# Value products of an attention tile: one block of 512 queries in place of two of 256

## The reference, cut to what matters

```python
logits = jnp.einsum('bhsd,bhtd->bhst', q, k) / (math.sqrt(Dh) * T)
att = jax.nn.softmax(logits, axis=-1)
out = jnp.einsum('bhst,bhtd->bhsd', att, v)
...
q = (jnp.einsum('bld,ed->ble', x, Wq) + bq).reshape(b, l, h, dh)
kv = (jnp.einsum('bmc,ec->bme', y, Wkv) + bkv).reshape(b, m, h, 2 * dh)
k, v = (kv[..., :dh], kv[..., dh:])
att = jax.nn.softmax(jnp.einsum('blhd,bmhd->blmh', q, k) * scale, axis=2)
out = jnp.einsum('blmh,bmhd->blhd', att, v).reshape(b, l, d)
```

## Time and profile before

| | |
|---|---|
| median of 3 runs | 1681.13 us (1680.69 to 1683.37) |
| profiled execution, span from first to last instruction | 1681.4 us |
| attention stage in it | about 130 to 1253 us |
| value products | x7424, 592.8 us busy, mean 391 ns |
| scores | x1856, 565.8 us busy, mean 382 ns |
| products for the maxima | x2048, 534.1 us busy, mean 358 ns |
| exponentials | x1856, 1001.7 us busy, mean 598 ns |
| maxima | x928, 1049.3 us busy, mean 1198 ns |

### The profile page before, as it was taken

The page is one execution under the profiler, slowest core; times in us unless marked ns, Lnnn a source line. Parts: engine busy times, 40 slices in busy tenths (PEclk is TensorE's granted clock), DMA queues, the critical chain, the costliest instruction groups (busy, mean ns, idle before and its releaser), DMA issues. The chain is left out here.

```text
span 1681.4 us, 36595 instructions
## 1 busy us (share of the span) xinstructions
PE 1598.4 (95%) x14449; PEld 634.1 (38%) x14452; DVE 1499.6 (89%) x2182; ACT 1319.1 (78%) x2590; POOL 406.3 (24%) x666
## 2 busy tenths in 40 slices
PE   6999999999999999999999999999989999889997
PEld 3542222222223232223322222222235555657774
DVE  6899999989999999989899999999948887688876
ACT  4618999879988989898899999999985565545544
POOL 5800110212223312312211111111013443533302
PEclk9999999999999999999999999999999999999999
DMA  4001001001101200101221011010002000015551
GB/s 147 14 7 20 14 14 14 14 14 22 31 14 21 45 14 14 33 17 27 70 55 26 14 21 20 14 27 14 14 28 63 1 1 1 1 31 95 101 102 51
DMA packets 148026, 52.32 MB, mean 31 GB/s; under 512 B 137424, under 2 KB 146128, under 8 KB 147600
## 3 DMA queue, kind: packets, MB, share of 16 engines
q1 hardware_dynamic: 147152, 48.62, 14.1%
q10 hardware_dynamic: 704, 1.38, 0.2%
HBM read 14.07 MB, written 2.10 MB: 10 GB/s over the span
## 5 line engine op out<-in xcount | busy, mean ns | idle before, releaser
L968 DVE TENSOR_REDUCE mxp<-ps_m 128x2 f32<-128x1024 f32 (+2 forms) x928 | 1049.3, 1198 | 41.3 <-PE ps_m L747 39.9
L897 ACT ACTIVATE work<-ps_s 128x512 f32<-128x512 f32 x1856 | 1001.7, 598 | 76.7 <-PE ps_s L771 48.9
L797 PE MATMUL ps_av<-work,vst 128*32 128x256 f32 x7424 | 592.8, 391 | 14.7 <-ACT avs L904 12.3
L771 PE MATMUL ps_s<-qb,k_stack 50*128 50x512 f16 x1856 | 565.8, 382 | 0.5 <-ACT v_rows L915 0.3
L747 PE MATMUL ps_m<-k_stack,qa 48*128 48x512 f16 (+1 forms) x2048 | 534.1, 358 | 2.3 <-PEq L1123 0.5
L797 PEld LDWEIGHTS ps_av<-work,vst 128*32 128x32 f32 x7424 | 147.0, 108 | 383.2 <-ACT work L897 321.6
L771 PEld LDWEIGHTS ps_s<-qb,k_stack 50*128 50x128 f16 x1856 | 119.7, 94 | 378.6 <-ACT work L897 323.4
L747 PEld LDWEIGHTS ps_m<-k_stack,qa 48*128 48x128 f16 x2048 | 108.2, 93 | 21.5 <-DVE mxp L968 14.8
L616 POOL TENSOR_SCALAR mtmp<-negm 128x16 f32<-128x16 f32 x32 | 8.2, 255 | 390.5 <-DVE negm L973 390.4
L602 POOL COPY vst<-v_rows 128x1024 f32<-128x1024 f32 (+1 forms) x32 | 30.6, 956 | 144.5 <-PE ps_av L797 144.5
L682 POOL TENSOR_TENSOR q_rows<-avs,rc 128x256 f32<-128x256 f32 x31 | 19.2, 619 | 173.3 <-DVE rc L979 173.3
(11 more groups left out here) (441 smaller groups left out, 2006.1 us busy)
## 6 DMA issues: line engine op xcount, KB each, us to landing
x_res<-in_x SPq DMA_DIRECT2D x4, 512.0 KB, 8.2
w_experts<-in_w_experts SPq DMA_DIRECT2D x1, 2048.0 KB, 8.0
out<-x_res SPq DMA_DIRECT2D x8, 256.0 KB, 2.2
v_rows<-in_ctx_c SPq DMA_DIRECT2D x1, 1664.0 KB, 7.3
work<-in_ctx_t SPq DMA_DIRECT2D x1, 1456.0 KB, 15.8
ctx_n<-in_ctx_n SPq DMA_DIRECT2D x1, 1248.0 KB, 8.0
w_qkv<-in_w_qkv ACTq DMA_DIRECT2D x1, 768.0 KB, 8.6
w_qkv<-in_w_qkv SPq DMA_DIRECT2D x1, 768.0 KB, 4.2
```

What stands on the lines that cost most here:

```text
L771: pe.matmul(ps_s[:, bank, :], STACKS[part(n)][rows, group(n) * PAIRS + j, t * P:t * P + P], qb[n % 2][rows, :, j, :], start=True, stop=Tru ...
L797: m = pe.matmul(ps_av[32 * h:32 * h + 32, cols], vst[n % 2][:, t, h, :], pbuf[(tau[n] + t) % 2][:, h, cols], start=(t == 0 and half == 0), ...
L897: a.activation(pbuf[g % 2][:, h, :], ps_s[:, b, :], ACT.Exp, scale=factor).then_inc(s["exp"], 1)
L968: v.tensor_reduce(dst, src, AX.X, ALU.max).then_inc(s["mred"], 1)
```

## The change

`values` loses its argument `half` and covers all 512 queries. The call between the two pairs of scores is gone; the call after the second pair remains. The semaphore `av` then counts one per tile in place of two, and every wait for it is adapted.

```diff
             def values(n):
 
                 k = keys_of(n)
                 if n >= 2:
-                    g.wait_ge(s["av"], 2 * tau[n - 1])
+                    g.wait_ge(s["av"], tau[n - 1])
...
-            def values(n, t, half):
+            def values(n, t):
 
                 pe.wait_ge(s["exp"], scored[n, t])
-                if t == 0 and half == 0:
+                if t == 0:
                     pe.wait_ge(s["vst"], n + 1)
                     if n > 0:
                         pe.wait_ge(s["avev"], n)
-                cols, end = slice(half * 256, half * 256 + 256), t == keys_of(n) - 1
                 for h in range(HG):
-                    m = pe.matmul(ps_av[32 * h:32 * h + 32, cols], vst[n % 2][:, t, h, :], pbuf[(tau[n] + t) % 2][:, h, cols],
-                                  start=(t == 0 and half == 0), stop=(end and half == 1))
+                    m = pe.matmul(ps_av[32 * h:32 * h + 32, :], vst[n % 2][:, t, h, :], pbuf[(tau[n] + t) % 2][:, h, :],
+                                  start=(t == 0), stop=(t == keys_of(n) - 1))
                 m.then_inc(s["av"], 1)
...
-                    values_behind(n, t, 0)
                     score(n, t, 1, tail)
-                    values_behind(n, t, 1)
-            values(NCH - 1, keys_of(NCH - 1) - 1, 0)
-            values(NCH - 1, keys_of(NCH - 1) - 1, 1)
+                    values_behind(n, t)
+            values(NCH - 1, keys_of(NCH - 1) - 1)
...
                 if h == 0 and g >= 2:
-                    a.wait_ge(s["av"], 2 * (g - 1))
+                    a.wait_ge(s["av"], g - 1)
...
-                a.wait_ge(s["av"], 2 * tau[n + 1])
+                a.wait_ge(s["av"], tau[n + 1])
```

More of the change, by code:

```diff
@@ L794, in values, with values_behind @@
                         pe.wait_ge(s["avev"], n)
-                cols, end = slice(half * 256, half * 256 + 256), t == keys_of(n) - 1
                 for h in range(HG):
-                    m = pe.matmul(ps_av[32 * h:32 * h + 32, cols], vst[n % 2][:, t, h, :], pbuf[(tau[n] + t) % 2][:, h, cols],
-                                  start=(t == 0 and half == 0), stop=(end and half == 1))
+                    m = pe.matmul(ps_av[32 * h:32 * h + 32, :], vst[n % 2][:, t, h, :], pbuf[(tau[n] + t) % 2][:, h, :],
+                                  start=(t == 0), stop=(t == keys_of(n) - 1))
                 m.then_inc(s["av"], 1)
-            def values_behind(n, t, half):
+            def values_behind(n, t):
                 if t > 0:
-                    values(n, t - 1, half)
+                    values(n, t - 1)
                 elif n > 0:
-                    values(n - 1, keys_of(n - 1) - 1, half)
+                    values(n - 1, keys_of(n - 1) - 1)
             def results(n):
```

## The result

The changed kernel takes 1743.2 us (median of 4 runs, 1741.7 to 1745.83) against 1681.75 of the kernel before in the same session. The ratio is 1.0367, 95% interval 1.0352 to 1.0382: slower by 61.5 us. The forecast was 1737, slower, range 1717 to 1762. The profiled execution has a span of 1739.9 us. In two of the runs further down one execution fell in a slower state (2085.7 us in `one_side_4b`, 1701.33 us in `before_one_side_4b`) and is left out of their times here.

A forecast was written before the change was run, and what follows sets the result against it. The prediction took a 2.38 us ring of waits per tile, with no engine full, as the bound; chunk-by-chunk differences summed to +56 us on 1681.13, giving 1737 us, range 1717 to 1762.

The forecast's parts named there:

- TensorE's block: A tile's wide value products, from their start to the next score's: 1.00 us, against two blocks of 0.57 before.
- The bounds, 0.93 to 1.07: Range for the wide value block's length in us, worth -20 to +25 us over some 420 tiles.
- the strips might not run side by side: Slower rival: column strips not fully parallel at 512 columns, 2.52 us a tile, 1796 us in all; chance 0.08.
- The ring: Loop of waits per tile: first exponential, s3, value block, next tile's s0, back to its exponential; 2.38 us.
- s3: Fourth score of a tile; with three score banks it waits for the tile's own first exponential.
- s0: First score of the next tile, standing behind the value block; 0.39 us, then 0.03 to its exponential.
- Two bounds within 2% of each other before: Ordinary tile of the kernel before: TensorE 2.22 us and VectorE 2.26 us, nearly equal.
- A chunk's first three intervals: Special tiles at the start of each chunk: 8.06 us after the change, about 7.8 before.
- Projection tiles: Tiles with extra projection products, taken as bound by TensorE's own work: 3.50 us after the change, 3.65 before.
- The wait of s3: Profile sign: s3's weight load comes 0.4 us after the previous score's pair has streamed, waiting for the first exponential.
- the collect distances: Profile sign: `collect` copies 39.0 us apart in plain self chunks, 31.9 in plain cross chunks.
- VectorE's idle: Profile sign: VectorE's idle time before its maxima rises from 39.8 to 96 us or so.

The follow-up runs named there:

- one_side_4b: Changed kernel without the odd heads' maxima products (VectorE reads the even heads' bank twice), scores through four banks instead of three: 1664.2 us, ratio 0.9901.
- before_one_side_4b: Kernel before, without the odd heads' maxima products (VectorE reads the even heads' bank twice), scores through four banks instead of three: 1676.97 us, ratio 0.9987.
- order_only: Kernel before, with both 256-column value blocks moved behind the second pair of scores, not widened: 1745.64 us, ratio 1.0381.
- half_columns: Changed kernel, value products of queries 256 to 511 left out in all tiles but a chunk's first: 1678.42 us, ratio 0.9981.
- one_side_3b: Changed kernel without the odd heads' maxima products (VectorE reads the even heads' bank twice), scores still through three banks: 1777.08 us, ratio 1.0568.
- wide_after_s2_units_last: Changed kernel, wide value block moved between a tile's third and fourth scores, both products of each maxima unit sent behind them: 1774.16 us, ratio 1.0546.
- short_maxima: Changed kernel, with half the columns left out of each of VectorE's maxima reductions: 1731.47 us, ratio 1.0294.
- before_short_maxima: Kernel before, with half the columns left out of each of VectorE's maxima reductions: 1656.53 us, ratio 0.9856.

## Why the prediction was right, point by point

- *TensorE's block* was put at 1.00 us, from today's 0.57 and 2 x 0.213; measured 1.00 (553.90 to 554.90). The bounds, 0.93 to 1.07, were not needed. That the strips might not run side by side fell with it.
- *The ring*, 2.38, measured 2.39. By legs: exponential 0.60, to the load 0.05 and to s3 itself 0.06, s3 to the block 0.32 where 0.31 was taken, block 1.00, s0 to the exponential 0.42. The order alone gives it (`order_only`), a shorter block ends it (`half_columns`), a fourth bank ends it (`one_side_4b`), 0.09 on one leg lengthens it by 0.09 (`one_side_3b`), another place keeps it at 2.39 (`wide_after_s2_units_last`), and VectorE's load does not touch it (`short_maxima`).
- *Two bounds within 2% of each other before*: `before_short_maxima` puts ordinary tiles at TensorE's 2.22. That was read from spacings of starts alone and held.
- *A chunk's first three intervals* were put at 2.55 + 3.13 + 2.38 = 8.06. Taken from whole chunks, 39.25 = 13 x 2.39 + 8.18, they are 0.1 too low, 3 us over 31 chunks.
- *Projection tiles* 3.50, measured 3.49, but with luck in it. The prediction has TensorE's own work bound them in both kernels. With VectorE short they take 3.31 and 3.45: in the changed kernel 0.18 of the 3.49, in the one before 0.20 of the 3.65, was VectorE's. The saving that was forecast, 0.14, is the difference of the two short ones; that the real tiles differ by 0.16 follows only because VectorE's share, which the prediction leaves out, is nearly the same in both.
- *Sum*: +56 forecast, +58.5 between the two profiled spans, +61.5 between the medians. The first of the 32 `collect` copies starts at 167.7 us before and at 169.1 after, the last at 1252.6 and 1313.4. So up to there the changed kernel took 60.8 us more, 5 over the forecast: 0.01 on some 420 ordinary tiles and 0.1 on 31 chunk starts give that and 2 more, within the rounding of such numbers. Behind the last copy it took 2.3 us less, and what is left lies between single executions and medians. Two lines of the sum are also added up low: 8 x 1.8 is 14.4 and not 14.2, and 4 x (44.0 - 42.85) is 4.6 and not 4.4, 0.4 us together.
- *Signs in the profile.* The wait of s3, the collect distances, the count of products and the clock came as listed. VectorE's idle was put at 96 us and is about 71. The error is in taking all added time for idle time: the group's busy time rose by 30 us as well (1078.9 from 1049.3) at almost the same mean, 1203 for 1198 ns. Reductions that follow each other closely overlap in the record (seven of 1.20 us in 8.01) and are counted once, spaced ones are not.
- *The two rules cited.* The Trainium skill says that larger matmuls are more efficient than smaller ones when possible ("Perfetto Trace Analysis", Optimizing Tensor Performance, Matmuls) and that a change of tiling mode drains the engine ("TensorEngine Tiling (Array Packing)", Key Properties). `order_only` agrees in part: the turn between products of different shape is all of TensorE's saving and the size next to nothing, 1.00 for 1.01 us. Neither rule decided the time, since the work that they save is not what the tile waits for.

## What to carry to other kernels

Before work on an in-order engine is merged into one longer block, walk each ring of waits once: the buffer's release, what stands behind the waiting instruction, and the way back. If its sum, with the block at its new length, is over the cadence of the fullest engine, the saving turns into a loss. Here one more buffer or a shorter block took it away again; less work for VectorE or another place for the block left the ring as it was. A merged block still paid in the steps where other work and not the ring set the pace, so try it there alone.

## What the runs showed of the hardware that was not expected

- With less work for TensorE its clock can fall. In `half_columns`, soon after the maxima products had ended and tiles ran 1.96 us apart, the granted clock went from 1.00 to 0.50, and the tiles to 2.84 us. The kernel before kept 1.00 and 2.13 us in the same chunk with twice the value columns. In chunks 4 and 5 the clock also fell, in `half_columns` (10 and 14 us at 0.50), `one_side_4b` (7 us) and `before_one_side_4b` (20 us), all of them with products left out; the kernel before and the changed one kept 1.00 there. `one_side_3b`, with maxima products left out too, did not fall, so less work alone does not decide it.
- Two waits that come together ahead of one weight load cost 0.08 us: 0.14 us from the end of the exponential to the product in `one_side_3b`, 0.06 with one wait in the changed kernel.
- Two value blocks of 256 columns back to back hold TensorE for 1.01 us, one of 512 columns for 1.00. Sixteen f32 products for eight made no difference as long as no product of another shape stood between them.
